# One perceiver block on one core: the gate's logits from transposed unnormalised tokens, and matmuls of ones in TensorE's waits

## The reference

```
x = x + xattn(layernorm(x), ctx, ctx, mask, ...)      # 16 heads, 257 keys per batch
x = x + attn(layernorm(x), Wq, bq, Wk, bk, Wv, bv)    # bind and unbind by FFT along the features
x = x + ffn(layernorm(x), W1, W2, Wg, bg)

def ffn(x, W1, W2, Wg, bg):                           # E = 8 experts, D = 512, H = 2048
    logits = xf @ Wg + bg                             # xf: 1024 tokens x 512
    one_hot = jax.nn.one_hot(jnp.argmax(logits, axis=-1), e)
    h = gelu(einsum('td,edh->eth', xf, W1))
    y = einsum('eth,ehd->etd', h, W2)
    return einsum('etd,te->td', y, one_hot)           # only the chosen expert counts

layernorm(x) = (x - mean) / sqrt(var + 1e-5)          # no gain and no bias
```

## Time and profile before

| what | us |
|---|---|
| median of 3 runs | 810.28 |
| the 3 runs | 810.23, 810.28, 2812.57 |
| the profiled execution, its time | 810.39 |
| the profiled execution, its span from first to last instruction | 808.3 |

### The profile page before, as it was taken

The page is one execution under the profiler, slowest core; times in us unless marked ns, Lnnn a source line. Parts: engine busy times, 40 slices in busy tenths (PEclk is TensorE's granted clock), DMA queues, the critical chain, the costliest instruction groups (busy, mean ns, idle before and its releaser), DMA issues.

```text
span 808.3 us, 22182 instructions
## 1 busy us (share of the span) xinstructions
PE 773.9 (96%) x8851; PEld 461.5 (57%) x8851; DVE 625.0 (77%) x990; ACT 470.1 (58%) x847; POOL 241.2 (30%) x413
## 2 busy tenths in 40 slices
PE   8987999999999999999999999996899999999995
PEld 3444455554455554455556545555868867876783
DVE  5877888888887887777768668787797879788860
ACT  4634656647665656665647034246478668766950
POOL 0143344332454333443322200004053323242220
PEclk9999999999999999999999999997799999999998
DMA  8335253444233443234423511102899998988500
GB/s 305 140 116 108 51 146 80 107 107 81 66 84 90 107 107 75 86 86 127 122 55 56 210 50 56 53 0 92 278 353 411 410 378 324 369 330 327 223 31 15
DMA packets 94901, 125.56 MB, mean 155 GB/s; under 512 B 76352, under 2 KB 79168, under 8 KB 83956
## 3 DMA queue, kind: packets, MB, share of 16 engines
q1 hardware_dynamic: 92260, 117.65, 45.6%
q0 software_dynamic: 2576, 7.02, 2.4%
HBM read 100.47 MB, written 6.88 MB: 133 GB/s over the span
## 4 chain that ended last, share of the span: by engine, by line
PE 79%; DVE 12%; ACT 3%; DMA 3%; issue 1%; POOL 1%; SPq 0%; POOLq 0%; DVEq 0%; ACTq 0%
PE bank L1470 58%; PE bank L1841 10%; PE bank L1632 4%; DVE arena L931 3%; PE bank L1813 3%; PE bank L1598 3%; ACT arena L696 2%; DMA arena<-arena 2%; DVE arena L987 2%; DVE arena L993 1%; ACT arena L663 1%; DMA arena<-in_wv_t 1%; DVE arena L1009 1%; PE bank L1800 1%; DVE arena L963 1%
## 5 line engine op out<-in xcount | busy, mean ns | idle before, releaser
L1470 PE MATMUL bank<-arena 128*128 128x160 f16 (+6 forms) x3992 | 572.7, 304 | 9.9 <-DVE arena L931 3.8
L1470 PEld LDWEIGHTS bank<-arena 128*128 128x128 f16 (+1 forms) x3992 | 327.8, 100 | 243.1 <-issue 12.0
L663 ACT ACTIVATE arena<-arena 128x256 f16<-128x256 f32 (+5 forms) x302 | 254.0, 889 | 23.6 <-PE bank L1813 10.1
L931 DVE SCALAR_TENSOR_TENSOR arena<-arena 128x2048 f16<-128x2048 f32 (+4 forms) x102 | 201.1, 1991 | 32.0 <-ACT arena L663 31.5
L663 ACT ACTIVATE arena<-bank 128x512 f16<-128x512 f32 (+1 forms) x175 | 100.1, 585 | 149.5 <-PE bank L1470 112.3
L931 DVE SCALAR_TENSOR_TENSOR arena<-bank,arena 128x512 f16<-128x512 f32 (+1 forms) x174 | 116.7, 682 | 48.3 <-ACT arena L663 44.7
L1841 PE MATMUL bank<-arena 128*128 128x512 f16 x384 | 86.6, 379 | 0.0
L696 ACT ACTIVATE arena<-arena 128x257 f32<-128x257 f32 x128 | 63.5, 498 | 26.3 <-DVE arena L995 26.3
L532 POOL TENSOR_TENSOR arena<-arena 32x1024 f16<-32x1024 f32 (+1 forms) x16 | 34.1, 2133 | 143.7 <-PE bank L1632 143.5
L1841 PEld LDWEIGHTS bank<-arena 128*128 128x128 f16 x384 | 36.2, 98 | 41.1
L549 POOL COPY arena<-arena 32x256 f16 (+1 forms) x128 | 50.3, 393 | 24.0 <-DVE arena L931 11.8
(11 more groups left out here) (110 smaller groups left out, 467.1 us busy)
## 6 DMA issues: line engine op xcount, KB each, us to landing
arena<-in_w SPq DMA_DIRECT2D x64, 1024.0 KB, 7.6
arena<-in_ctx_t SPq DMA_DIRECT2D x15, 1024.0 KB, 5.5
arena<-in_awt SPq DMA_DIRECT2D x3, 1024.0 KB, 7.1
l_dram<-arena SPq DMA_DIRECT2D x4, 512.0 KB, 3.8
x_dram<-arena SPq DMA_DIRECT2D x1, 2048.0 KB, 14.4
arena<-in_wk_t SPq DMA_DIRECT2D x4, 256.0 KB, 4.9
arena<-in_ctx_t SPq DMA_DIRECT2D x4, 256.0 KB, 5.7
arena<-in_wv_t SPq DMA_DIRECT2D x1, 1024.0 KB, 8.7
```

The lines of the kernel that those rows point to most:

```text
L663: return a.activation(dst, src, ACT.Copy, scale=scale)
L931: return v.scalar_tensor_tensor(dst, src, scale, h, ALU.mult, ALU.subtract)
L1470: last = m.matmul(out_ap, w, x, start=(n == 0), stop=(n == len(pairs) - 1))
```

## The change

It does these things:

1. `gate_transpose(t)` takes the tiles of `x_tok` in float32 (4 transposes) as soon as `x2_done` stands at t + 1. `gate(t)` is 4 float32 products of the transposed tile `x2T` with the float32 gate weights `wg_stage`. The logits come from `rstd * product + (shift * column sums of Wg + bg)` on VectorE; the column sums come from 8 products of ones with the halves of Wg (`gate_column_sums`).
2. All 8 tiles are normalised on ScalarE (`l2_split`), from `shift` that GpSimd now makes for groups 4, 5 and 6; all low halves are made on GpSimd. VectorE's `normalise` of groups 4 and 6 and its two `l2_lo` go.
3. VectorE's `piece_lo(0, 3)` moves from behind group 6 to ahead of `bind(1, 1)`.
4. On TensorE the transposes of tiles 0 to 3 and the column sums move between the two parities of `back` of tiles 4 to 7; the gates and transposes of tiles 4 to 7 alternate in another order.
5. TensorE does 4 matmuls of ones (128 x 512) between the logits and the wait for the one-hot choice, and 5 between the counts and the wait for the permutation. `first_gather` now waits for `l2_lo` of all tiles as well.
6. In the first round the order of `first_gathered`, `slots(own_rank)` and `piece_lo(0, 5)` changes.

```diff
 # GpSimd
-            for n in range(2, 5):
+            def l2_shift(n):
                 power(n)
+                ts = slice(LN_GROUPS[n][0], LN_GROUPS[n][-1] + 1)
+                pool.wait_ge(s["ln_rstd"], n + 1)
+                g.tensor_tensor(shift[:, ts], minus_mean[:, ts], rstd[:, ts], ALU.mult).then_inc(s["l2_shift"], 1)
+            power(2)
+            power(3)
+            l2_shift(4)
             pool.wait_ge(s["unbound"], 4)
             for t in LN_GROUPS[4]:
                 l2_lo(t)
-            power(5)
+            l2_shift(5)
             l2_lo(LN_GROUPS[5][0])
+            l2_shift(6)
             l2_lo(LN_GROUPS[5][1])
-            power(6)
+            for t in LN_GROUPS[6]:
+                l2_lo(t)
 # ScalarE
             def l2_split(t):
-                if t in LN_GROUPS[5]:
-                    act.wait_ge(s["l2_normal"], t - HT + 1)
-                else:
-                    act.wait_ge(s["ln_out"], 2 * NT + (t + 1 if t < HT else t - 1))
+                act.wait_ge(s["l2_shift"], 1 + (t >= HT) + (t >= HT + 2))
+                a.activation(l2_f[:, t, :], x_tok[:, t, :], ACT.Identity, bias=shift[:, t:t + 1],
+                             scale=rstd[:, t:t + 1]).then_inc(s["l2_normal"], 1)
+                act.wait_ge(s["l2_normal"], t + 1)
                 hi(l2_tile(0, t), l2_f[:, t, :], 1.0).then_inc(s["l2_hi"], 1)
...
             act.wait_ge(s["unbound"], 4)
             gate_transpose_out(HT)
+            gate_transpose_out(HT + 1)
+            l2_split(HT)
+            gate_transpose_out(HT + 2)
+            l2_split(HT + 1)
+            gate_transpose_out(HT + 3)
             l2_split(HT + 2)
-            gate_transpose_out(HT + 1)
             l2_split(HT + 3)
 # VectorE
             lo(wg_hl[1], wg_stage, SG, wg_hl[0]).then_inc(s["wg_split"], 1)
-            normalise(4, l2_f)
+            piece_lo(0, 3)
             bind(1, 1)
             unbind(1, 0)
             unbind(1, 1)
...
-            normalise(6, l2_f)
-            dve.wait_ge(s["l2_lo"], HT + 2)
-            for t in LN_GROUPS[6]:
-                l2_lo(t)
-            piece_lo(0, 3)
...
+            v.tensor_tensor(gate_base, by_tile(gate_sums), by_expert(shift), ALU.mult).then_inc(s["chain_dve"], 1)
             dve.wait_ge(s["logits_ps"], 1)
             v.scalar_tensor_tensor(
-                logits, BC[:, 0:NT * E].rearrange("p (t e) -> p t e", e=E), 1.0 / (SX * SG), by_tile(bg_bc),
-                ALU.mult, ALU.add).then_inc(s["chain_dve"], 1)
+                logits, BC[:, 0:NT * E].rearrange("p (t e) -> p t e", e=E), 1.0 / SX, by_expert(rstd),
+                ALU.mult, ALU.mult).then_inc(s["chain_dve"], 1)
+            dve.wait_ge(s["chain_dve"], next(chain))
+            v.tensor_tensor(gate_base, gate_base, by_tile(bg_bc), ALU.add).then_inc(s["chain_dve"], 1)
+            next(chain)
+            dve.wait_ge(s["chain_dve"], next(chain))
+            v.tensor_tensor(logits, logits, gate_base, ALU.add).then_inc(s["chain_dve"], 1)
...
-                    first_gathered(0)
-                    first_gathered(1)
+                    for c in range(KC):
+                        first_gathered(c)
+                    slots(own_rank)
                     piece_lo(0, 5)
-                    first_gathered(2)
-                    first_gathered(3)
-                    slots(own_rank)
 # TensorE
             def gate_transpose(t):
-                pe.wait_ge(s["l2_lo"], t + 1)
+                pe.wait_ge(s["x2_done"], t + 1)
                 pe.wait_ge(s["lt_done"], from_zero(t - 1))
...
+                for c in range(KC):
+                    last = m.transpose((BG, BH)[t % 2][:, c * P:(c + 1) * P], x_tok[:, t, c * P:(c + 1) * P], ident)
             def gate(t):
                 pe.wait_ge(s["lt_done"], t + 1)
-                return product(BC[:, t * E:(t + 1) * E],
-                               [(l2T[:, t, u, c, :], wg_hl[z][:, c, :]) for c in range(KC)
-                                for u, z in ((0, 0), (0, 1), (1, 0))])
+                return product(BC[:, t * E:(t + 1) * E], [(x2T[:, t, c, :], wg_stage[:, c, :]) for c in range(KC)])
+            def keep_clock(times):
+                for _ in range(times):
+                    m.matmul(BF[:].rearrange("p (c x) -> p c x", c=KC), ones16, ones16.unsqueeze(1).broadcast_to((P, KC, P)),
+                             start=True, stop=True)
...
             for t in range(HT, NT):
                 back(t, 0)
+            for t in range(HT):
+                gate_transpose(t)
+            gate_column_sums()
             for t in range(HT, NT):
                 back(t, 1).then_inc(s["irfft_ps"], 1)
-            for t in range(HT):
-                gate_transpose(t)
-            pe.wait_ge(s["wg_split"], 2)
-            pe.wait_ge(s["spec_done"], 24)
             for t in range(HT):
                 gate(t)
             gate_transpose(HT)
             gate_transpose(HT + 1)
+            gate(HT)
             gate_transpose(HT + 2)
-            gate(HT)
+            gate(HT + 1)
             gate_transpose(HT + 3)
-            for t in range(HT + 1, NT):
-                last = gate(t)
-            last.then_inc(s["logits_ps"], 1)
+            gate(HT + 2)
+            gate(HT + 3).then_inc(s["logits_ps"], 1)
+            pe.wait_ge(s["x2_done"], NT)
+            keep_clock(WAIT_FILLERS[0])
             pe.wait_ge(s["onehot_done"], 1)
...
             def first_gather():
+                keep_clock(WAIT_FILLERS[1])
                 pe.wait_ge(s["perm_done"], 2)
+                pe.wait_ge(s["l2_lo"], NT)
+WAIT_FILLERS = (4, 5)
```

More of the change, by code:

```diff
@@ L126, in perceiver_block @@
         rstd = keep.take([NT], F32)
+        minus_mean = keep.take([NT], F32)
         score_sums = keep.take([PAIRS], F32)
@@ L152, in perceiver_block @@
         onehot16 = keep.take([NT, E], F16)
+        gate_sums = keep.take([E], F32)
+        gate_base = keep.take([NT, E], F32)
         top, top2 = (keep.take([NT], F32) for _ in range(2))
@@ L278, in perceiver_block @@
         ea = Region(spec_off, after_spec)
-        l2T = ea.take([NT, 2, KC, P], F16)
+        x2T = ea.take([NT, KC, P], F32)
         hid_hl = [ea.take([FC, CAP], F16) for _ in range(2)]
@@ L870, in _ @@
                 gate_transpose_out(t)
-            act.wait_ge(s["l2_shift"], 1)
-            for t in LN_GROUPS[5]:
-                a.activation(l2_f[:, t, :], x_tok[:, t, :], ACT.Identity, bias=shift[:, t:t + 1],
-                             scale=rstd[:, t:t + 1]).then_inc(s["l2_normal"], 1)
-                l2_split(t)
             act.wait_ge(s["unbound"], 4)
             gate_transpose_out(HT)
+            gate_transpose_out(HT + 1)
[3 more added lines that the diff above has]
+            gate_transpose_out(HT + 3)
             l2_split(HT + 2)
-            gate_transpose_out(HT + 1)
             l2_split(HT + 3)
-            gate_transpose_out(HT + 2)
-            gate_transpose_out(HT + 3)
             for k in range(4, PIECES - 2):
@@ L1285, in x2 @@
                 return v.bn_stats(stats[:, t, :], x_tok[:, t, :])
-            def l2_lo(t):
-                dve.wait_ge(s["l2_hi"], t + 1)
-                v.tensor_tensor(l2_tile(1, t), l2_f[:, t, :], l2_tile(0, t), ALU.subtract).then_inc(s["l2_lo"], 1)
             piece_lo(0, 0)
@@ L1310, in _ @@
             unbind(1, 1)
-            for n, (t, u) in ((5, LN_GROUPS[5]), (6, LN_GROUPS[6])):
+            for t, u in LN_GROUPS[5:]:
                 x2(t)
@@ L1719, in gate_transpose @@
             def gate_transpose(t):
-                pe.wait_ge(s["l2_lo"], t + 1)
+                pe.wait_ge(s["x2_done"], t + 1)
                 pe.wait_ge(s["lt_done"], from_zero(t - 1))
-                bank = (BG, BH)[t % 2][:].bitcast(F16)
-                for n in range(2):
-                    for c in range(KC):
-                        slot = n * KC + c
-                        last = m.transpose(bank[:, slot * P:(slot + 1) * P], l2_tile(n, t)[:, c * P:(c + 1) * P], ident16)
+                for c in range(KC):
+                    last = m.transpose((BG, BH)[t % 2][:, c * P:(c + 1) * P], x_tok[:, t, c * P:(c + 1) * P], ident)
                 last.then_inc(s["lt_ps"], 1)
```

18 lines of the change are left out of this document (12 added, 6 removed).

## The result

| | before | changed |
|---|---|---|
| median of 14 runs each | 810.71 us | 813.01 us |
| smallest run | 810.23 us | 812.28 us |
| ratio, 95% interval | 1 | 1.0034, 1.0024 to 1.0044 |
| profiled execution, its span | 810.39, 808.3 us | 813.07, 811.1 us |
| start of the experts | 577.46 | 581.56 |

The changed kernel is 2.3 us slower by the medians, 2.8 by the ratio (0.0034 x 811). That is no change by 2%, but the interval excludes 1. The forecast was 811.4, inside a range of 807.0 to 817.5. Three of the changed kernel's 14 executions took 816.6 to 817.3 us at a mean granted clock of 0.978, the other eleven, the profiled one among them, 812.3 to 813.7 at 0.982 to 0.984, and this is why the ratio gives more than the medians; no trace shows one of the three.

What follows compares the result with a forecast made beforehand. Bound: engine-to-engine hand-overs at about 540 to 577 us, which set the experts' start. Logits +1.4, two steps +0.5, half-clock gates +0.5, gather clock -1.4 make +1.0 on 810.39: forecast 811.4 us, range 807.0 to 817.5.

Steps and rivals of the forecast that it cites:

- Step 5: One-hot to experts: matmuls of ones bring the clock back, gather -1.4 us; half clock in the last two gates +0.5.
- Step 1: VectorE ahead of `bind(1, 1)`: early `piece_lo(0, 3)` makes it 3.5 us late, 2.8 stay; ScalarE's longer `l2_split` is hidden.
- Step 2: TensorE between the parities of `back`: four transposes and the column sums make the second parity 5.5 us late.
- Step 3: VectorE's `x2`: the last one ends at 561.6, 4.8 us late.
- Step 4: Last `x2` to logits: gate record 0.119 us, logits 1.4 us later; two more VectorE steps make +1.9 at the one-hot.
- Step 6: Weights: 4 MB start 7 us later; ScalarE's wait grows by perhaps 3 us, hidden, up to 1 us if not.
- Order of the copies: VectorE behind the gather: copies come at once instead of behind `piece_lo(0, 4)` and `(0, 5)`; worth nothing.
- C: Faster rival: the delay from `piece_lo(0, 3)` and the transposes between parities doesn't arise; 806 to 808 us, chance 0.08.
- D: Slower rival: matmuls of ones fail, clock stays at half through the whole gather; 814.5 us, chance 0.1.
- A: Slower rival: the gate is bound by its weight loads, 190 ns or more a record; 813 to 820 us, chance 0.2.
- B: Faster rival: the gate costs 0.5 us a tile and the clock holds; 807.5 us, chance 0.17.

Runs made afterwards that it cites:

- r1: Changed kernel with `piece_lo(0, 3)` on VectorE back behind the `x2` of tiles 6 and 7; 1.0021 of the kernel before.
- r14: Kernel before with only `piece_lo(0, 3)` moved ahead of `bind(1, 1)`; 1.0053 of the kernel before, 4.3 us slower.
- r2: Changed kernel with the transposes of tiles 0 to 3 and the column sums back behind the second parity of `back`; 1.0034 of the kernel before.
- r4: Changed kernel with gate weights repeated eight times, 64 moving columns for 8, seven of eight results unread; 0.9993 of the kernel before.
- r6: Changed kernel with scaled logits left in PSUM, so VectorE's sum with `gate_base` has one SBUF operand; 1.0025 of the kernel before.
- r15: r13 with the change's order of the copies (four copies and `slots(own_rank)` ahead of `piece_lo(0, 5)`); 0.9973 of the kernel before.
- r13: Kernel before with only the 4 and 5 matmuls of ones added at the same two places; 0.9981 of the kernel before.
- r9: r4 with 11 and 8 matmuls of ones instead of 4 and 5; 0.9977 of the kernel before.
- r11: r10 with the edits of r2 and r6 as well; 0.9950 of the kernel before.
- r10: r9 with `piece_lo(0, 3)` back and ScalarE's `l2_split` of tiles 0 to 3 behind the last spectrum; 1.0011 of the kernel before.
- r12: r11 with last four copies ahead of `l2_split`, transposes ahead of gates, last shift ahead of low halves, `piece_lo(0, 3)` behind `gate_base`; 0.9958 of the kernel before.

## Why the prediction was nearly right, and what was mis-sized

The direction and the place were right, and the start of the experts was forecast 1.7 us too early: 1.6 us are missing at the logits and 0.8 at the choice, and the gather gave 0.5 more than forecast. The term of the sum that was mis-sized is step 5's "+0.5 (half clock in the gates)".

- **Step 1** held: the wait ahead of L941 was forecast at about 4 us and is 4.01; `bind(1, 1)` was forecast 3.5 us late and was 3.4. The last spectrum's copy, forecast for about 544.2, ends at 544.22 in before's clock (544.97 + 0.69 - 1.44), and `unbind(1, 1)` began at 545.29 (forecast 545.3). That the 2.8 us is the price of `piece_lo` holds only for the sum of both delays: r1 gave 1.05 back, while on the kernel before, without the pairs, r14 shows 2.8 beside the clock.
- **Step 2** held, 5.2 for 5.5 us. What it did not say is that this delay costs nothing by itself: r2 removed 2.4 us of it without gain.
- **Step 3** held, 4.3 for 4.8.
- **Step 4**: the record was 0.104 us at full clock, between the taken 0.119 and the lower bound. The Trainium skill's LDWEIGHTS rule ("TensorE: Matmul & The Clock Gate", LDWEIGHTS (loading the stationary operand)), 107 ns, was nearer than my row, as long as the clock was full; at the 1.2 GHz level the record took 0.214. So at full clock the gates are even a little cheaper than I had them, and in r4 the logits are level with before's. The path was right at full clock too: there the last gate waits 0.51 us for ScalarE's copy of tile 7, which stands behind the pair of tile 5, as the sum had it. In the changed kernel, at half clock, TensorE's own queue ends later, and it is the path.
- **Step 5** failed in its size, and by its own numbers. I let the clock fall 4.8 us after the last `back`, at 560.4, and had gate 4 begin at 560.7 (finer windows of before put its fall at 554.66, 4.6 us after, and its return 5.7 us into the gather, for my 5.9). So all four late gates and two of their transposes were behind the fall, but I charged half clock for "the last two" and took a quarter of that. The clock fell at 560.2, 558.8 in before's clock, and behind it lay the four gates and nearly all of their four transposes. r4, where the clock held and little else differed, puts the price at 3.5 us at the logits. Against it stood -1.9 in the gather for the -1.4 taken. The two more steps on VectorE were as many as forecast, but one of them met GpSimd, which is the other 0.8 us at the one-hot; r6 removed all but 0.3 of it.
- **Step 6** held in its outcome. The weights start later, as forecast (piece 7 is issued at 572.50, before at 564.75). ScalarE's waits for DMA are 1.43 us at 603.19 and 1.13 at 606.23, together 0.6 us more than the 1.93 before and not 3; and from the start of the experts to the end the changed kernel is no longer than before (the -1.3 above).
- **Order of the copies**: "Nothing" was right only for the changed kernel's late gather. On the kernel before with fillers it is worth 0.7 us by the ratios, whose intervals overlap, and 1.1 in the traces (r15 against r13). The prediction misread the change here: the copies don't come at once, `piece_lo(0, 4)` stands ahead of them in both kernels (575.67 in the changed trace, the first copy at 577.87).
- **Rivals**: C did not arise. D did not either: the clock came back within the gather. A's time, 813 to 820, contains the result, but its mechanism, dear loads at full clock, is not what the runs show (0.104 us). B's clock needed r9's edits.

What stays open: why the clock falls behind those gates, beyond that 64 columns prevent it; why r2's profiled execution lies 1.9 us off its ratio; and how r4's 3.3 us divide between clock and gather beyond what its one trace shows.

## What to carry to other kernels

Work moved ahead of a bottleneck to shorten a later stage is paid in the queue where it lands: here the shortened path was worth 2.5 us at the logits (r11), and what was moved for it cost nearly as much, and came back only when all of it was undone (r10 against r11). Price a new kind of matmul at both clock levels, and read the granted clock over the stretch that it makes, not only behind idle time. Where one engine's wait is shortened, look for the order on the next one that it uncovers (r13) before judging the change by its time.

## What the hardware showed that I had not expected

- The granted clock fell while TensorE's busy column was full. Behind 32 float32 records of 8 columns, 0.104 us apart, it went from 1.00 to 0.50; with 64 columns at the same spacing it stayed at 1.00 through the gates (r4, r9). The Trainium skill ("TensorE: Matmul & The Clock Gate", Why this matters for your kernels) names idle gaps between bursts of matmuls as what to avoid. r14's and r10's traces agree (3.73 us idle, then 0.59; 2.49 idle, then 0.59); the changed kernel's rows show a fall with no gap.
- A float32 record bound by its weight load slows with the clock: 0.104 us at the full level, 0.214 at half, and 8 or 64 moving columns cost the same (0.83 and 0.84 us a tile).
- A small VectorE step with both operands in SBUF waits for a GpSimd step that runs: 0.22 us became 0.55 to 1.09 (r4, r6, r12), and the other way round GpSimd's step of two columns went from 0.70 to 2.67 beside a VectorE step of 2.28 (r10). One operand in PSUM ended it (r6, 0.23).
- One early DMA issue of SyncE, the same in all kernels, took between 0.43 and 1.29 us from run to run and shifted the changed kernel's whole trace with it.
